# Turning the first layer's rows with 32x32 block transposes and 16 SBUF copies instead of TensorE transposes

## What is computed

```python
xn = layernorm(x)                                   # (4096, 256)
# attention part: chunks of 32 rows, no softmax, a fixed decay mask
S = (xn Wq^T)(xn Wk^T)^T * mask
att = (sigmoid(xn Wg^T) * (S (xn Wv^T))) Wo^T + xn
# expert part: all 16 experts of width 128, weighted by a sigmoid
ffn = sum_e sigmoid(xn sel_e) * relu(xn keys[e]) values[e]
x = x + att + ffn
# second layer: four gated linear scans (top 2 mixed), and one of 8 experts per row
```

## Time and profile before

| | us |
|---|---|
| median of 3 runs | 1049.42 |
| lowest, highest | 1047.63, 1049.46 |
| span of the profiled execution, first to last instruction | 1046.4 |

### The profile page before, as it was taken

The page is one execution under the profiler, slowest core; times in us unless marked ns, Lnnn a source line. Parts: engine busy times, 40 slices in busy tenths (PEclk is TensorE's granted clock), DMA queues, the critical chain, the costliest instruction groups (busy, mean ns, idle before and its releaser), DMA issues. The chain is left out here.

```text
span 1046.4 us, 20027 instructions
## 1 busy us (share of the span) xinstructions
PE 1035.6 (99%) x6626; PEld 927.9 (89%) x6626; DVE 754.9 (72%) x1233; ACT 629.5 (60%) x1186; POOL 333.8 (32%) x291
## 2 busy tenths in 40 slices
PE   8999999999999999999999999999999999999998
PEld 7998888989889898898877888899999999888887
DVE  5875756656575566857779998876777777588887
ACT  4554445444444444545566666788888888566665
POOL 3353453444444344353452772000000000373000
PEclk9999999999999999999999999999999999999999
DMA  5216111010111201423156275588887876552203
GB/s 176 78 36 221 41 41 60 0 69 31 40 60 40 76 24 41 173 70 141 33 212 262 80 268 205 177 269 262 266 282 241 276 246 225 198 173 98 80 21 101
DMA packets 75139, 141.12 MB, mean 135 GB/s; under 512 B 9936, under 2 KB 43088, under 8 KB 74064
## 3 DMA queue, kind: packets, MB, share of 16 engines
q1 hardware_dynamic: 66320, 126.45, 35.5%
q0 software_dynamic: 3072, 8.39, 2.3%
q10 hardware_dynamic: 5696, 5.64, 1.6%
HBM read 101.86 MB, written 38.60 MB: 134 GB/s over the span
## 5 line engine op out<-in xcount | busy, mean ns | idle before, releaser
L775 POOL TENSOR_TENSOR acc<-acc,ytmp 128x512 f32<-128x512 f32 x120 | 156.5, 1304 | 248.2 <-ACT ytmp L870 227.1
L1572 ACT ACTIVATE act_o<-ps,scan_bias 128x512 f32<-128x512 f32 x189 | 129.7, 688 | 100.0 <-PE ps L388 95.8
L870 ACT ACTIVATE ytmp<-ps,sel 128x256 f32<-128x256 f32 x256 | 107.4, 471 | 99.8 <-PE ps L1104 99.1
L940 DVE SCALAR_TENSOR_TENSOR hT_l<-ps,hT_h 128x512 fp32r<-128x512 f32 x128 | 87.7, 685 | 104.8 <-ACT hT_h L829 104.6
L1102 PE MATMUL ps<-vals_h,hT_h 128*128 128x256 f32 x512 | 145.1, 283 | 0.8 <-DVE hT_l L940 0.7
L1103 PE MATMUL ps<-vals_l,hT_h 128*128 128x256 f32 x512 | 143.6, 280 | 0.0
L1104 PE MATMUL ps<-vals_h,hT_l 128*128 128x256 f32 x512 | 143.6, 280 | 0.0
L829 ACT ACTIVATE hT_h<-ps 128x512 fp32r<-128x512 f32 x128 | 76.3, 596 | 98.8 <-PE ps L388 98.6
L1724 POOL DMA_INDIRECT late_y<-y_d,pos_i x20 | 23.2, 1158 | 273.8 <-DMA y_d<-y_sb 268.0
L1896 DVE TENSOR_TENSOR_SCAN h_b<-a_b,hstate,xs_b 128x512 f32<-128x512 f32 x63 | 88.1, 1398 | 30.4 <-ACT a_b L1579 27.0
L386 PE MATMUL ps<-xT_h,keys_h 128*128 128x512 f32 x256 | 104.9, 410 | 1.2 <-DVE xT_l L427 1.2
(11 more groups left out here) (249 smaller groups left out, 2765.3 us busy)
## 6 DMA issues: line engine op xcount, KB each, us to landing
raw<-w SPq DMA_DIRECT2D x78, 512.0 KB, 5.3
x1T<-xT_d SPq DMA_DIRECT2D x16, 512.0 KB, 5.2
comb_b<-comb_d SPq DMA_DIRECT2D x8, 1024.0 KB, 7.4
w_small<-w SPq DMA_DIRECT2D x14, 512.0 KB, 5.0
xs_d<-zeros ACTq DMA_DIRECT2D x1, 4992.0 KB, 19.2
x_d<-x SPq DMA_DIRECT2D x8, 512.0 KB, 4.4
xn_d<-xn SPq DMA_DIRECT2D x8, 512.0 KB, 2.7
xT_d<-nT_h SPq DMA_DIRECT2D x8, 512.0 KB, 2.7
```

What stands on the lines that cost most here:

```text
L775: pool.tensor_tensor(dst[:, 2:4, :], acc[:, 2:4, :], ytmp[:, k % 2, :, :], ALU.add).then_inc(acc23, 1)
L870: act.activation(ytmp[:, k % 2, j - 2, :], yb(k, j), ACT.Copy, scale=sel[:, j, k:k + 1]).then_inc(y_23, 1)
L1572: act.activation(act_o[:, i % 2, w, :], ps[:, 3 * (i % 2) + w, :], func, bias=scan_bias[:, w, i:i + 1]).then_inc(act_g, 1)
```

## The change

For groups 2 to 8 the rows are no longer transposed on TensorE. DVE transposes each 128x256 tile of `xn` in 32x32 blocks into `y0` (the memory of `v32`, which is free by then), 2 tiles at k = 8 and 2 at k = 9. Then SP issues 16 transfers from SBUF to SBUF, one for each pair of partition quadrants, each 32 partitions x 8 pieces of 128 bytes, which put the blocks where a full transpose has them, in `xT`. ACT and DVE make `xT_h` and `xT_l` out of `xT` at the same steps as before, and both operands of DVE's subtraction now lie in SBUF. POOL's addition into `xT` goes (it stays in group 1). `bn_aggr` and `rstd` move from k = 7 to 6, and `ln_norm` from k = 9, 10 to k = 8, 9.

```diff
+    def turn_blocks(dve, dst, src, tiles, done):
+        for j in tiles:
+            dve.transpose(dst[:, :, :, j, :], src[:, j, :].rearrange("p (c b a) -> p b c a", c=DC, b=N_Q)).then_inc(done, 1)
+
+    def move_blocks(sp, dst, src, done):
+        for b in range(N_Q):
+            for q in range(N_Q):
+                to, of = slice(b * Q32, (b + 1) * Q32), slice(q * Q32, (q + 1) * Q32)
+                sp.dma_start(dst[to].rearrange("a c (j q r) -> a (c j) q r", j=JT, q=N_Q)[:, :, q, :],
+                             src[of, b].rearrange("a c j r -> a (c j) r")).then_inc(done, 16)
...
+            def move_x(g):
+                wait_alone(sp, y0_ok, JT * (g + 1))
+                move_blocks(sp, xT, y0, xT_in)
...
             with sp.Fori(1, GROUPS - 2) as g:
                 body(g, False, False)
+                move_x(g)
...
-                    if k == 0:
-
-                        pool.wait_ge(side_free, 2 if first else freed(g, "v01") - 1)
-                        if not first:
-                            pool.wait_ge(side_full, use(g, "v01"))
+                    if k == 0 and first:
+                        pool.wait_ge(side_free, 2)
                         pool.tensor_tensor(xT[:], xT_h[:].bitcast(F32), xT_l[:].bitcast(F32), ALU.add).then_inc(xT_sum, 1)
...
-                    if k == 7 and not last:
+                    if k == 6 and not last:
                         rstd(pool, mv0, stats0[:, :, 0], rstd0, mvs0, pe0, rs0, g + 1)
...
-            def xT_hi(g, c, first):
-
-                t_hi(act, use(g, "t0", first) + c, xT_h[:, c, :], ps[:, 6 + c, :])
+            def xT_hi(g, c):
+
+                act.wait_ge(xT_in, MOVED * (g + 1))
+                act.activation(xT_h[:, c, :], xT[:, c, :], ACT.Copy).then_inc(xT_hi_ok, 1)
...
-            def xT_lo(nh, c):
-                lo_of(dve, nh + c, xT_l[:, c, :], xT_h[:, c, :], ps[:, 6 + c, :])
+            def xT_lo(g, c):
+                dve.wait_ge(xT_hi_ok, DC * g + c + 1)
+                dve.tensor_tensor(xT_l[:, c, :], xT[:, c, :], xT_h[:, c, :].bitcast(F32), ALU.subtract).then_inc(xT_ok, 1)
...
-                    if k == 7 and not last:
                         ln_aggr(dve, stats0, mv0, bn0, mvs0, g + 1)
-                    if k in (9, 10) and not last:
-                        if k == 9:
+                    if k in (8, 9) and not last:
+                        tiles = range(2 * (k - 8), 2 * (k - 7))
+                        if k == 8:
                             dve.wait_ge(acc_ip, g + 1)
-                        ln_norm(dve, xn, x_in, mv0, rstd0, rs0, xn0, g + 1, range(2 * (k - 9), 2 * (k - 8)))
+                        ln_norm(dve, xn, x_in, mv0, rstd0, rs0, xn0, g + 1, tiles)
+                        dve.wait_ge(xn0, JT * (g + 1) + 2 * (k - 7))
+                        turn_blocks(dve, y0, xn, tiles, y0_ok)
...
-                        if k == 0:
-                            pe.wait_ge(side_free, xT_ready - 1 + c)
+                        if k == 0 and first:
+                            pe.wait_ge(side_free, 1 + c)
+                        if k == 0 and not first:
+                            pe.wait_ge(xT_ok, DC * (g - 1) + c + 1)
...
                     if k == E0 - 3:
-                        if not last:
-                            pe.wait_ge(xn0, JT * (g + 2))
                         pe.wait_ge(o_23, g + 1)
                         pe.wait_ge(acc01, N01 * g + 2 * (O_STEP + 1) + 1)
                         if last:
                             mixture_transpose(pe, mix1, 1, 6).then_inc(side_full, 1)
-                        else:
-                            transposes(pe, xn, 0).then_inc(side_full, 1)
-                    if k == E0 - 2 and not last:
-                        transposes(pe, xn, 1).then_inc(side_full, 1)
```

More of the change, by code:

```diff
@@ L51 @@
 CHUNK = 32
+Q32 = 32
 NL = M + E1
@@ L133, in build @@
     otmp = sig_g[:, 0, :].rearrange("p (j d) -> p j d", j=2)
+    N_Q = P // Q32
+    MOVED = 16 * N_Q * N_Q
+    y0 = v32[:].rearrange("p j (k r) -> p (j k) r", r=Q32).rearrange("p (b c j) r -> p b c j r", b=N_Q, c=DC)
     stats0 = ra("stats0", [P, JT, 6], F32)
@@ L328, in build @@
     xT_sum = sem("xT_sum")
+    y0_ok, xT_in, xT_hi_ok, xT_ok = sem("y0_ok"), sem("xT_in"), sem("xT_hi_ok"), sem("xT_ok")
     sel_ok = sem("sel_ok")
@@ L347, in build, with hi_use @@
     O_STEP = 11
-    USES = ["v01", "v23", "q", "g", "s", "t1", "lg", "o", "lt", "op", "t0", "t0b"]
+    USES = ["v01", "v23", "q", "g", "s", "t1", "lg", "o", "lt", "op"]
     POST = ("t1", "lg", "lt")
-    HI_USES = ["t1", "t0", "t0b"]
     def use(g, name, first=False):
         names = [u for u in USES if not (first and u in POST)]
-        start = 2 if first else 12 * g - 1
+        start = 2 if first else 10 * g - 1
         return start + names.index(name)
[L360 to L363, removed]
+    def hi_use(g, name):
+        return 2 + g - 1
     def freed(g, name, first=False):
         names = [u for u in USES if u != "op" and not (first and u in POST)]
-        start = 2 if first else 11 * g - 1
+        start = 2 if first else 9 * g - 1
         return start + names.index(name) + 1
@@ L374, in post_use @@
             n = 2 + POST.index(name)
[L375 removed]
+            return use(g, "op") + n, hi_use(g + 1, "t1"), freed(g, "lt") + n
         return use(g + 1, name), hi_use(g + 1, "t1"), freed(g + 1, name)
@@ L722, in _ @@
                 weight(name)
+            move_x(GROUPS - 2)
             for i in range(N_LATE):
@@ L858, in body @@
                     if k == E0 - 2 and not last:
-                        act.wait_ge(xT_sum, g + 1)
-                        xT_hi(g, 0, first)
+                        xT_hi(g, 0)
                     if k == E0 - 1 and not last:
-                        xT_hi(g, 1, first)
+                        xT_hi(g, 1)
                     act.wait_ge(y_f23, E0 * g + k + 1)
@@ L967, in body @@
                     if k == E0 - 2 and not last:
-                        xT_lo(hi_use(g, "t0", first), 0)
+                        xT_lo(g, 0)
                     if k == E0 - 1 and not last:
-                        xT_lo(hi_use(g, "t0", first), 1)
+                        xT_lo(g, 1)
                     dve.wait_ge(y_f01, E0 * g + k + 1)
@@ L1055, in _ @@
             for c in range(DC):
-                xT_lo(0, c)
+                lo_of(dve, c, xT_l[:, c, :], xT_h[:, c, :], ps[:, 6 + c, :])
             split("v")
@@ L1129, in values @@
                     last_mm.then_inc(side_full, 1)
-                xT_ready = 2 if first else freed(g, "v01") - 1
                 up(0)
@@ L1157, in body @@
                         ready("g")
-                        pe.wait_ge(xT_sum, g + 1)
+                        if first:
+                            pe.wait_ge(xT_sum, 1)
                         for j in range(JT):
```

1 line of the change is left out of this document (added).

## The result

| | before | changed |
|---|---|---|
| median us (lowest to highest), 4 runs each | 1048.53 (1047.46 to 1049.46) | 1063.34 (1062.22 to 1063.95) |
| span of the profiled execution | 1046.4 | 1062.1 |

The account below looks back on a forecast made before the run. TensorE, busy 99%, was taken as the bound. Per group -0.87 + 1.65 + 1.06 = +1.84 us, over 7 groups +12.9, added to 1049.4 gave 1062.3 us; range 1055.5 to 1077.

Parts of the forecast that it names:

- What goes: TensorE, twice a group: four transposes and the longer hold of the matmul behind them go, -0.87 us per group.
- Step 8: Between oT_l and relu_lo(10): two ln_norm, a wait and two block transposes, all uncovered, +1.65 us per group (1.6 to 2.1).
- the second set at step 9: The ln_norm and block transposes at step 9 stay just hidden: down(11) comes at 188.3 and needs 188.2.
- The group's end: POOL's step 14 addition holds the second half's xT_l, so TensorE waits before up(0)'s second half, +1.06 us per group.
- TensorE would arrive 0.43 earlier, since the second four transposes are gone: Group's end: TensorE reaches the matmuls needing xT_l at 202.06, relative to xT_l, and waits until 203.12.
- In 7 groups, the same in all: The +1.84 us per group applies equally in groups 1 to 7, +12.9 us in total.
- The transfers: SP's 16 issues after step 9, 0.45 us each, land before ACT's xT_h at step 14, 3.8 us to spare.
- An issue over 0.69: Sign against the prediction: SP's transfers taking over 0.69 us per issue, where the 3.8 us of slack is used up.
- The rival of late transfers: SP's transfers reach ACT late: 1075 us at 0.8 us per issue, 1094 at 0.97; chance 0.17.
- POOL doesn't hold `xT_l`: Group's end costs only 0.26 us, +1.04 per group, +7.3 in all, 1056.7 us; chance 0.10.
- POOL holds the block transposes too: Step 8: block transposes start only after POOL's step 9 addition, +0.9 us there, +6.3 in all, 1068.6 us; chance 0.10.
- The saving stays: Both waits, at step 8 and the group's end, stay hidden: 6.1 us gained, 1043.3 us; chance 0.05.

Follow-up runs that it names:

- e5_both: Changed kernel, but tiles 0 and 1 normalised and turned at step 7, both halves of xT_h and xT_l made at step 14; ratio 0.9962 to the kernel before.
- e4_step7: Changed kernel, but ln_norm and block transposes of tiles 0 and 1 at step 7, tiles 2 and 3 at step 9; 1049.22 us, ratio 1.0014 to the kernel before.
- e1_pair: Changed kernel, but both halves of xT_h and xT_l made at step 14, ahead of POOL's addition; 1058.27 us, ratio 1.0095 to the kernel before.
- e2_dve_first: Changed kernel, but POOL's addition of step 14 waits until the second xT_l is written; 1059.06 us, ratio 1.0105 to the kernel before.
- e5_again: The e5_both kernel measured once more, on another chip; ratio 0.9957 to the kernel before.
- e6_32_moves: Changed kernel with the same bytes and pieces in 32 transfers of 16 KB in place of 16; 1136.64 and 1150.39 us, ratio 1.0699 to the kernel before.
- e7_o_first: The e5_both kernel, but POOL's addition of step 8 waits until oT_l is written; ratio 0.9940 to the kernel before.

## Why the prediction was right, and where its sizes were off

1062.3 us were forecast, 1063.34 measured. The two mechanisms of the sum, the wait at step 8 and the one at the group's end, held. That the sum came out this close is in part luck. Inside a group a wait that was missed made up for two that were taken too large, which leaves the five groups of the loop 0.3 under the forecast; groups 1, 7 and 8 cost 4.0 more than forecast, the second layer gave 0.8 back, and the kernel before, measured again, had a median 0.9 lower. Against that median the change costs 15.2 us, where 12.9 were forecast.

- *What goes, -0.87 a group.* Held: the loop of `e5_both`, where only this and the wait at `down(15)` are left, gives -0.54 = -0.87 + 0.33.
- *Step 8, +1.65.* Mechanism right, size 1.44 in the trace and 1.45 by `e4_step7`. The block transposes take 0.70 between starts, 0.80 was taken; the wait for an own result, 0.1, is not to be seen beside the pair of `ln_norm` (0.76 with it). That the second set at step 9 is hidden held: there is no wait at `down(11)`, which starts 1.45 after `relu_lo(11)` where 0.80 is needed.
- *The group's end, +1.06.* GpSimd holds `xT_l` as said: `e1_pair` and `e2_dve_first` each take the wait away. Its size is 0.84 in the trace, 0.80 and 0.78 by these two. It ends 0.55 after GpSimd's end, as forecast, but TensorE arrives later than it was taken to, for it had waited just before.
- *Missed: `down(15)`, +0.33.* The step "TensorE would arrive 0.43 earlier, since the second four transposes are gone" asked only what is late at `up(0)`. What had stood behind the transposes, `down(15)`, comes first, and its `relu_lo(15)` had been on time only by their cover. The two terms of the end together are 1.17, which is why 1.06 looked right.
- *Sum of a group.* -0.87 + 1.44 + 0.33 + 0.84 = +1.74, measured +1.78, forecast +1.84.
- *"In 7 groups, the same in all".* This failed. Group 1 cost 4.49 and groups 7 and 8 together 3.17, 7.7 in place of 3.7. In group 1 GpSimd's addition falls on the pair of `ln_norm` (1.74 for 0.73); the prediction took the price from a pair in group 3 that meets it at the edge only (0.90), though the next pair of that group, at 186.26, has it in full (1.60). In group 7 `WB_l` meets the addition. Both waits pass 2 us, and in this trace the granted clock is at 0.50 behind both, which no term foresaw. `e4_step7`, without these waits, has neither fall. Of the 4.49 the clock is about 1.55, by `e1_pair` and `e2_dve_first`; the rest is the longer wait.
- *The transfers: hidden, 0.45 an issue.* Hidden, yes, but at 0.66 an issue in groups 3 to 6, near the 0.69 at which it was said to turn, and past it in groups 1 and 2, at 0.70 and 0.73. An issue over 0.69 was to show the prediction wrong; no wait came of it, by 0.28 us in group 2. The row taken as nearest, 0.47 for a store of weights, was not near. The rival of late transfers (chance 0.17) was closer to the truth than its chance says: with both mendings it came true in one group of `e5_again`, and `e6_32_moves` shows what it would have cost in every group.
- *The rivals.* "POOL doesn't hold `xT_l`" fell by `e1_pair` and `e2_dve_first`. "POOL holds the block transposes too" fell: all 28 lie between 0.40 and 0.45 us, 12 of them (one pair in each of groups 2 to 7) beside an addition of GpSimd, in group 3 from 189.47 with the addition from 189.24. That it is `ln_norm` which GpSimd can hold, shown by `e7_o_first`, was there in its argument, "already slowed beside POOL", but not drawn out to a price. "The saving stays" fell for the change as made; of the 6.1 us that it named, `e5_both` gets 3.2 in the first layer and `e5_again` 2.7.
- The second layer gives back 0.84 us, which is not explained. It is the size of the spread between runs.

The rule of the Trainium skill, "SBUF — State Buffer", section "Who interferes with whom", on which the end of the group rested, was borne out by three edits here (`e1_pair`, `e2_dve_first`, `e7_o_first`) as far as VectorE comes second; no run here shows GpSimd coming second and waiting. The estimate by the Trainium skill, "VectorE: DVE Perf Modes", section "The three transpose paths", 1.24 a pair, was too high: a pair takes 0.70.

## What to carry to other kernels

What is taken off the busiest engine is gained only where nothing else makes it wait. The same work on VectorE cost 1.44 us at step 8 and nothing at steps 7 and 9, so the first question of such a change is which step has the slack. When something is taken out of an engine's list, ask of every instruction behind it whether what it needs was on time only thanks to the cover. And work out the first and the last pass of a loop by their own rows: they made up half of the loss here.

## What was unexpected of the hardware

- A transfer from SBUF to SBUF with 32 partitions on each side holds SP's queue for 0.60 to 0.66 us, whether it has 256 pieces of 128 bytes or 128; the loads of `x_in` and the stores of rows shown above hold it for 0.34 to 0.64. It lands after 1.9 us in the median, and after 3.8 at most (in `e5_again`).
- A transpose of 128x256 f32 in 32x32 blocks takes 0.40 to 0.45 us on VectorE and is not held by GpSimd's addition, while `ln_norm` (one tensor operand and two per-partition scalars, f32) is when it starts just behind one: 1.38 to 1.43 us for 0.40 in all seven groups of `e7_o_first`.
- TensorE's granted clock fell to 0.50 behind an idle time of 2.46 us in three traces (the changed kernel, `e1_pair`, `e6_32_moves`) and not in a fourth (`e2_dve_first`), and behind one of 2.09 us in three and not in a fourth (`e6_32_moves`). It stayed at 1.00 behind those of 1.42 and 1.67. A fall cost about 1.55 us.
